# Graph attention on one core: group 1's values go into the banks of its own t, and group 0's transposes are split, reordered and paired

## The reference

```
h      = max(layernorm(x), 0)
out    = h @ weight;   q = h @ wq;   k = h @ wk
alpha  = max(q @ k^T, 0) * (adj != 0)
alpha  = softmax(alpha, axis=1)            # over the rows n of alpha[n, m]
result = x + alpha @ out
```

## Time and profile before

| | |
|---|---|
| median of 3 runs | 421.62 us (420.26 to 421.87) |
| the profiled execution, its own time | 420.8 us |
| span of its trace, first to last instruction | 419.0 us |
| PE busy | 406.6 us, 97% |
| DVE, ACT, POOL busy | 68%, 60%, 71% |

### The profile page before, as it was taken

The page is one execution under the profiler, slowest core; times in us unless marked ns, Lnnn a source line. Parts: engine busy times, 40 slices in busy tenths (PEclk is TensorE's granted clock), DMA queues, the critical chain, the costliest instruction groups (busy, mean ns, idle before and its releaser), DMA issues.

```text
span 419.0 us, 9187 instructions
## 1 busy us (share of the span) xinstructions
PE 406.6 (97%) x3499; PEld 314.8 (75%) x3499; DVE 282.9 (68%) x504; ACT 253.3 (60%) x517; POOL 298.2 (71%) x315
## 2 busy tenths in 40 slices
PE   5999997999999999999999999999999999999996
PEld 4434543779889797979889797979889797978452
DVE  4786566475866768685876768676777677456353
ACT  4478774657485666667485666667586765523421
POOL 0379887979979797979879797979889796130320
PEclk9999999999999999999999999999999999999999
DMA  7965748996969797896978598996988599261022
GB/s 286 364 91 97 194 81 212 202 219 177 191 216 178 221 165 206 199 210 178 196 238 157 154 213 219 194 207 180 187 251 151 157 228 221 51 107 59 0 103 100
DMA packets 157368, 73.97 MB, mean 177 GB/s; under 512 B 131216, under 2 KB 139408, under 8 KB 157328
## 3 DMA queue, kind: packets, MB, share of 16 engines
q1 hardware_dynamic: 156752, 72.37, 75.5%
q10 hardware_dynamic: 576, 1.05, 0.7%
HBM read 24.12 MB, written 16.78 MB: 98 GB/s over the span
## 4 chain that ended last, share of the span: by engine, by line
PE 81%; POOL 9%; DMA 3%; DVE 3%; ACT 1%; SPq 1%; issue 1%; DVEq 0%; POOLq 0%; ACTq 0%
PE bank L1041 9%; PE bank L1027 9%; PE bank L1026 9%; PE bank L1042 9%; PE bank L1024 9%; PE bank L1039 9%; PE s_bank L1055 3%; PE s_bank L1053 3%; PE s_bank L1054 3%; POOL hn_lo L375 2%; PE bank L1060 2%; PE bank L1062 2%; PE bank L1061 2%; DMA x_sb<-in_x 2%; POOL hn_lo L401 2%; PE bank L1160 2%
## 5 line engine op out<-in xcount | busy, mean ns | idle before, releaser
L375 POOL TENSOR_TENSOR hn_lo<-h,hn_hi 128x512 f16<-128x512 f32 x64 | 73.4, 1159 | 41.0 <-ACT hn_hi L512 40.7
L502 ACT ACTIVATE h<-x_sb,shift,rstd 128x512 f32<-128x512 f32 x64 | 49.8, 803 | 51.4 <-POOL shift L370 51.4
L401 POOL TENSOR_TENSOR hn_lo<-s,hn_hi 128x512 f16<-128x512 f32 x52 | 58.6, 1159 | 0.0
L1024 PE MATMUL bank<-hT_hi,mt_hi 128*128 128x256 f16 x208 | 56.7, 273 | 0.0
L1027 PE MATMUL bank<-hT_hi,mt_lo 128*128 128x256 f16 x208 | 56.7, 273 | 0.0
L1041 PE MATMUL bank<-wt_lo,hT_hi 128*128 128x256 f16 x208 | 56.7, 273 | 0.0
L1042 PE MATMUL bank<-wt_hi,hT_lo 128*128 128x256 f16 x208 | 56.7, 273 | 0.0
L1026 PE MATMUL bank<-hT_lo,mt_hi 128*128 128x256 f16 x208 | 56.7, 273 | 0.0
L1039 PE MATMUL bank<-wt_hi,hT_hi 128*128 128x256 f16 x208 | 56.7, 273 | 0.0
L517 ACT ACTIVATE hn_hi<-s 128x512 f16<-128x512 f32 x52 | 32.5, 628 | 36.4 <-POOL s L390 23.9
L407 POOL TENSOR_TENSOR probs<-exps,row_inv 128x512 f32<-128x512 f32 x16 | 16.8, 1049 | 47.3 <-DVE row_inv L829 47.3
(11 more groups left out here) (142 smaller groups left out, 1153.4 us busy)
## 6 DMA issues: line engine op xcount, KB each, us to landing
x_sb<-in_x SPq DMA_DIRECT2D x16, 1024.0 KB, 5.5
out_h<-x_sb SPq DMA_DIRECT2D x64, 256.0 KB, 2.1
adj_sb<-in_adj SPq DMA_DIRECT2D x16, 256.0 KB, 5.4
w_sb<-in_L_gnn_weight SPq DMA_DIRECT2D x1, 1024.0 KB, 11.4
hn_lo<-in_L_gnn_wk ACTq DMA_DIRECT2D x2, 256.0 KB, 3.9
hn_lo<-in_L_gnn_wk SPq DMA_DIRECT2D x2, 256.0 KB, 3.7
hn_hi<-in_L_gnn_wq SPq DMA_DIRECT2D x2, 256.0 KB, 6.3
hn_hi<-in_L_gnn_wq ACTq DMA_DIRECT2D x2, 256.0 KB, 6.9
```

What stands on the lines that cost most here:

```text
L375: nc.gpsimd.tensor_tensor(hn_lo[:, s, b], h[:, b], hn_hi[:, s, b], ALU.subtract).then_inc(h_split, 1)
L401: nc.gpsimd.tensor_tensor(low, s32[:, f], high, ALU.subtract).then_inc(s_split, 1)
L502: nc.scalar.activation(h[:, b], x_sb[:, s, b], ACT.Relu, bias=shift[:, b:b + 1], scale=rstd[:, b:b + 1]).then_inc(h_made, 1)
L1024: nc.tensor.matmul(o, bh[:, k, cols], ah[:, :, k], start=first and c == 0 and k == 0, stop=False, skip_group_check=True)
```

## The change

Three edits. First, group 1's values go to `M_BANK`, the banks where its t was; PE awaits each bank's `t_split` (the low part of t has been taken) before it writes v there, and `out_read` only ahead of scores(1); `period(2)` starts when seven of the eight values have been split. Second, SP awaits only the high part of h of graphs 0 and 1 to transpose it, then the low part; graphs 2 and 3 are transposed as a pair, high parts in one DMA and low parts in another. Third, on ACT the high part of t(1, 3) is made before those of the sums S2 and S4 of group 2, no longer after them.

```diff
-        V_BANK = [bank[VB][:], bank[VE][:], bank[FREE][:], bank[TA][:]]
+        def v_bank(g):
+            return M_BANK if g == 1 else [bank[VB][:], bank[VE][:], bank[FREE][:], bank[TA][:]]
...
-        hT0_landed = [sem(f"hT0_landed{b}") for b in range(GB)]
+        hT0_landed = [sem(f"hT0_landed{b}") for b in range(3)]
...
-            def transpose_first(b):
-                sp.wait_ge(h_split, b + 1)
-                sp.dma_start_transpose(hT_hi[:, 0, b], hn_hi[:, 0, b]).then_inc(hT0_landed[b], 16)
-                sp.dma_start_transpose(hT_lo[:, 0, b], hn_lo[:, 0, b]).then_inc(hT0_landed[b], 16)
+            def transpose_first(b, n, landed):
+                sp.wait_ge(h_hi_made, b + n)
+                sp.dma_start_transpose(hT_hi[:, 0, b:b + n].rearrange("p b k n -> p (b k) n"),
+                                       hn_hi[:, 0, b:b + n].rearrange("p b d -> p (b d)")).then_inc(landed, 16)
+                sp.wait_ge(h_split, b + n)
+                sp.dma_start_transpose(hT_lo[:, 0, b:b + n].rearrange("p b k n -> p (b k) n"),
+                                       hn_lo[:, 0, b:b + n].rearrange("p b d -> p (b d)")).then_inc(landed, 16)
...
-            for b in range(GB):
-                transpose_first(b)
+            transpose_first(0, 1, hT0_landed[0])
+            transpose_first(1, 1, hT0_landed[1])
+            transpose_first(2, 2, hT0_landed[2])
...
-            act.wait_ge(hT0_landed[3], 2 * 16)
             hi_of_h(2, 0, 3)
...
             hi_of_whole_t(1, 2)
+            hi_of_whole_t(1, 3)
             hi_of_sum(2, 0, 2, S2)
             hi_of_sum(2, 0, 3, S4)
-            hi_of_whole_t(1, 3)
             hi_of_whole_v(1, 0)
...
-            pe.wait_ge(hT0_landed[GB - 1], 2 * 16)
             pe.wait_ge(m_split, K)
...
-            pe.wait_ge(t_split, K + 1)
             for b in range(GB):
-                pe.wait_ge(out_read, b + 1)
+                pe.wait_ge(t_split, K + b + 1)
                 whole_product_v(1, b)
+            pe.wait_ge(out_read, GB)
             scores(1, 1, quadrants=False)
-            pe.wait_ge(v_split, 2 * GB)
+            pe.wait_ge(v_split, GB + TE + 1)
```

More of the change, by code:

```diff
@@ L601, in hi_of_whole_v @@
                     act.wait_ge(out_filled, GB * g)
-                nc.scalar.activation(v_hi[:, b], V_BANK[b], ACT.Copy, scale=T_SCALE).then_inc(v_hi_made, 1)
+                nc.scalar.activation(v_hi[:, b], v_bank(g)[b], ACT.Copy, scale=T_SCALE).then_inc(v_hi_made, 1)
             def hi_of_whole_t(g, c):
@@ L873, in lo_of_whole_v @@
                 vec.wait_ge(v_hi_made, GB * g + b + 1)
-                nc.vector.scalar_tensor_tensor(v_lo[:, b], V_BANK[b], T_SCALE, v_hi[:, b], ALU.mult,
+                nc.vector.scalar_tensor_tensor(v_lo[:, b], v_bank(g)[b], T_SCALE, v_hi[:, b], ALU.mult,
                                                ALU.subtract).then_inc(v_split, 1)
@@ L1143, in whole_product_v @@
             def whole_product_v(g, b):
-                s, dst = g % 2, V_BANK[b]
+                s, dst = g % 2, v_bank(g)[b]
                 for k in range(K):
```

## The result

The changed kernel takes 422.19 us in the median (421.61 to 422.71, 22 runs), the kernel before 421.38 us (420.26 to 422.13, 22 runs). The ratio is 1.0018, with a 95% interval of 1.0012 to 1.0025: slower by 0.2%, as small as predicted, and measurable only because there were so many runs. The profiled execution of the changed kernel took 422.03 us with a span of 420.2, the one of the kernel before 420.8 with 419.0. Lines after the change lie 7 or 8 higher: L409 is the old L401, L984 the old L977.

The account below looks back on a forecast made before the run. POOL's chain to p_lo(1), not PE, was taken as the bound: +1.35 (three L401) - 0.29 (layernorm scales) - 0.2 (earlier start) = +0.86 us, giving 422.5 us against the median 421.62; range 419.8 to 423.6 for 8 times in 10.

Parts of the forecast that it names:

- Part 1: Banks of v(1): removes PE waits of 2.67 and 0.40 us, worth 0 on the chain to the end.
- What bounds: POOL's chain from normalise(0) to p_lo(1) sets outs(1); the end moves by what p_lo(1) moves; PE's waits are covered.
- Part 2: Transposes: PE gains 1.0 us at v(0, 2), POOL's chain 0.2 us, bounds 0 and 1.0.
- the lower bound of the prediction: SP's queue: issuing a pair of transposes costs between 1.27 us (as one) and 2.54 us (as two).
- With a normal landing: Pair's DMA: landing normally, it leaves over half a microsecond to spare, so PE gains 1.0 us.
- Part 3: ACT's order: mt_lo start at 63.4 beside POOL's L401; three L401 lengthen, +1.35 us, layernorm scales change by -0.29.
- The price: Each mt_lo meeting a POOL L401 lengthens POOL's next by 0.45 us, bounds 0 and 0.68.
- The count: Group 2's L401 on POOL: numbers 2, 3 and 4 are lengthened, the first mt_lo falling inside the first.
- The sum: shift(3): +1.35 - 0.29 - 0.2 = +0.86 us, moving outs(1) from 89.75 to about 90.6 and the end with it.
- Free meetings: Rival: mt_lo beside POOL's L401 don't meet or cost POOL nothing; 420.5 us, or 419.7; chance 0.20.
- PE's waits as the bound: Rival: POOL has room, so PE's 4.1 us of waits come out in full; 417.5 us; chance 0.08.
- The pair lands late: Rival: the paired low transpose lands 1 us after 31.27, normalise(0) slips 1 us; 423.7 us; chance 0.12.

Follow-up runs that it names:

- e8: Changed kernel with graphs 2 and 3 transposed singly, four mt_lo held behind POOL's layernorm scales, two wt_lo moved earlier: 419.61 us, ratio 0.9954 to the kernel before.
- e2: Kernel before with only the four mt_lo held back behind POOL's layernorm scales of group 3: 421.35 us, ratio 0.9999.
- e4: Kernel before with only ACT's new order, t(1, 3)'s high part ahead of the sums S2 and S4: 423.27 us, ratio 1.0042.
- e9: Kernel before with only the new transposes, high parts first and graphs 2 and 3 as a pair: 421.53 us, ratio 1.0007.
- e6: Kernel before with only the new banks for v of group 1 and PE's waits for them: 421.20 us, ratio 1.0004.
- e1: Changed kernel with the four mt_lo held back behind POOL's layernorm scales of group 3: 420.61 us, ratio 0.9982 to the kernel before.
- e3: Changed kernel with ACT's old order, t(1, 3)'s high part behind the sums S2 and S4: 421.05 us, ratio 0.9998 to the kernel before.
- e7: Changed kernel with graphs 2 and 3 transposed each by itself, high parts still first: 421.12 us, ratio 1.0004 to the kernel before.
- e5: Changed kernel with the old first transposes, new banks and ACT order kept: 421.45 us, ratio 1.0010 to the kernel before.
- e10: Changed kernel with unpaired transposes and two of the four mt_lo held behind POOL's layernorm scales: 420.63 us, ratio 0.9987 to the kernel before.

## Why the prediction was right

Time and sign came out, and so did the mechanism on POOL, with one term too large and one missing. That the median fits as well as it does is in part luck: Part 1's zero holds only while PE keeps its full clock.

**What bounds.** Right for the profiled executions: `outs(1)` follows p_lo(1) by 0.05 us in both kernels, and what stands behind it takes PE the same 324.82 us. The waits that went from PE (2.67 and 0.40) came back as 2.17, 0.67 and a longer stand at `outs(1)`. e8, whose POOL chain is 0.62 shorter than that of the kernel before, is faster. In e2, e4 and e9, though, whose clock fell in mid-stream, PE was the last at `outs(1)`.

**Part 1, worth 0.** Right at full clock: in e6 `outs(1)` is at 90.10, not earlier than 89.75, and the 0.35 later are the lost first place of L367. What the prediction left out is what such a wait can do in other executions: in the profiles of e2 and e9 the granted clock falls behind it, and PE is as late as POOL at `outs(1)`, or later. There, removing the wait has a value ("Against the median" and the last section).

**Part 2, 1.0 us for PE and 0.2 for the chain.** The chain's 0.21 fits by luck. Counted from the first high part of h, `normalise(0)` comes 0.38 earlier, and all profiles agree: 35.86 to 35.95 us in the five with the old transposes, 35.48 in the four with the pair. The changed kernel's profile merely started 0.18 later. The softmax shift still takes 0.58 us (0.54 before), beside POOL as the prediction had it. PE's 1.0 didn't come: it restarts at 31.06 instead of 31.32, 0.44 earlier when counted from the same point. The queue of SP and the chain of waits in the changed kernel, 18 to 32 us:

```profile
24.79 1.31 SPq L281 DMA_TRANSPOSE hT_hi<-hn_hi  x1
26.14 1.34 SPq L284 DMA_TRANSPOSE hT_lo<-hn_lo  x1
```

```profile
26.14 4.88 DMA hT_lo<-hn_lo
```

A pair costs one issue (1.34, the lower bound of the prediction), so it is issued 1.00 us earlier than in the earlier trace rows, but lands 4.88 us later instead of 4.12. "With a normal landing" was the wrong assumption, 0.76 us slower (4.62 to 4.64 us in e1, e3 and e9, against 4.12 to 4.44 for the same transpose without the pair). It didn't matter, since PE's microsecond was hidden in any case.

**Part 3, +1.35 and -0.29.** The price was right: 1.61 - 1.16 = 0.45 for each L409 that follows an `mt_lo`. The count was wrong. I put the first `mt_lo` at 63.4 inside the first L401, which ends at 63.5; it came at 63.73, inside the second, since the low part of t(1, 3) waited for ACT until 60.48 and not 60.2. So two were lengthened, +0.90, and two `mt_lo` were left for the scales, which stayed at 2.96 (+0.02) instead of losing 0.29. The sum is 0.92 against 1.06 foreseen. e7, where the `mt_lo` come 0.3 us earlier against POOL's stream, has the three (+1.38) and the scales at 2.64 (-0.30) of the prediction, and the chain longer by 1.04.

The Trainium skill (SBUF — State Buffer, "Who interferes with whom") was right that a VectorE `tensor_tensor` with two inputs in SBUF contends with GpSimd's reads. The price by its whole duration would be 0.68 for each; the traces show 0.45, for the loop's kind as for this one.

**The sum.** `outs(1)` moved by +0.66 (foreseen +0.86), or by +0.48 without the 0.18 by which this profile started late: +0.87 on the chain, -0.38 ahead of it. The 0.59 at the end stood in no step: I had written that the end moves by what p_lo(1) moves. In the profiles that makes +1.26 against +0.9.

**Against the median.** Here another error offset the missing 0.59. The timed executions beside the experiments have their mean granted clock on record. Of the 29 of the kernel before that ran beside e1 to e4, 10 ran at 1.000, with a median of 420.6 us, and 19 at 0.994 to 0.996, with 421.5. Beside e5 to e8 the two kinds have 420.9 and 421.4, beside e9 and e10 421.0 and 421.4. The profile that I read was of the first kind (clock 1.000, 420.8 us). The changed kernel has both kinds too, 15 of 22 at 0.994 to 0.997, but they are no slower: 422.18 against 422.24 at full clock. So against executions at full clock the change costs 1.2 to 1.7 us, against the more frequent others 0.7 to 0.8, and the medians differ by 0.81. The clocks of the 22 executions of the kernel before that this last number rests on aren't on record.

**The rivals.** Free meetings: refuted by 1.61 and by e1. PE's waits as the bound: refuted at full clock, by e6 and by the 1.03 us that PE now waits for p_lo(1); where the clock fell behind `out_read`, PE was the bound, by 0.62 us in e9. Of the 4.1 us that this rival named, less than one was at stake in such executions. The pair lands late: true of the DMA, not of `normalise(0)`.

## What to carry to other kernels

Before an edit that lets an engine start earlier, write down what the other engines do at its new time: here an instruction with two SBUF operands on DVE cost POOL's chain 0.45 us a meeting, and putting it behind the neighbour's critical stretch (e1, e8) made a faster kernel of it (e8, which also drops the pair and moves two `wt_lo`: 0.46% below the one before). A wait removed from PE is worth what the chain behind the next join allows, in this kernel nothing at full clock; a covered wait can still cost, when the granted clock falls behind it. Times from the start of a span are compared between two profiles only after a look at an instruction ahead of all edits. An effect of half a microsecond needs the ends of both traces compared, not only the place of the edit.

## What the runs showed that I had not expected

**The granted clock falls after a wait in mid-stream.** In e2, PE stood still for 2.65 us in its wait for `out_read`; first PE's timeline, then the windows of e2:

```profile
65.89 0.38 PE L1151 MATMUL bank<-w_hi,hT_hi 128*128 128x512 f16 x1 [2.65 <-DVE x_sb L833]
```

```profile
65.00:68.00 3.00, 2.11 (x8) 0.95 (x9) 3.00 (x6) 0.00 (x0) 3.00 (x5) 0.82 1.01 178
68.00:71.00 3.00, 3.00 (x10) 1.07 (x9) 0.23 (x2) 0.76 (x2) 1.58 (x4) 0.61 0.79 150
```

In 68 to 71 us PE makes 10 matmuls instead of 14 (at half clock they start 0.43 us apart, otherwise 0.22) and the mean clock is 0.61: part of the stretch ran at the lower level, 1.2 GHz. In e4 the wait was 4.15 us, first in PE's timeline and then by windows:

```profile
80.21 0.40 PE L1024 MATMUL bank<-hT_hi,m_hi 128*128 128x256 f16 x1 [4.15 <-DVE v_lo L874]
```

```profile
80.00:83.00 3.00, 2.79 (x14) 1.99 (x15) 1.68 (x4) 0.63 (x1) 2.92 (x3) 0.50 1.11 333
83.00:86.00 3.00, 3.00 (x17) 2.19 (x16) 1.29 (x2) 2.90 (x10) 3.00 (x4) 0.54 1.26 276
```

Here it fell while PE still stood (77 to 80 us: 0.82). Four more profiles have such a stretch: e9 behind a wait of 2.98 us for `out_read`, and e3, e7 and e10 behind waits of 2.00, 2.60 and 2.05 us before `period(2)`. First e9, then e7, by windows:

```profile
65.00:68.00 3.00, 3.00 (x9) 1.12 (x8) 3.00 (x6) 0.00 (x0) 2.92 (x5) 0.53 0.66 140
```

```profile
79.00:82.00 3.00, 3.00 (x19) 2.26 (x18) 1.78 (x4) 0.63 (x1) 2.92 (x3) 0.62 1.14 311
```

These six executions have a mean clock of 0.992 to 0.996 on record, the six profiled ones without such a stretch 0.999 or 1.000, though three of them have waits of 2.67, 2.17 and 2.12 us (before, after, e5). So the same wait does it in some executions and not in others, and a mean of 0.996 or less marks those where it did.

What it costs depends on where it falls. Behind `out_read` (e2, e9) PE takes 25.24 and 25.20 us from v(1, 0) to `outs(1)` without a wait, in the kernel before 24.42 with 0.56 of waits in it: PE becomes the bound, and by these numbers the kernel before would reach `outs(1)` 0.8 us later in such an execution (my estimate; the two kinds of its executions differ by 0.9, 0.5 and 0.4 us in the three sets). Before `period(2)` (e3, e7, e10) it costs nothing: PE waited another 0.47 to 0.49 us at `outs(1)`, which still follows p_lo(1) by 0.05 or 0.06. The changed kernel has its longest wait, 2.17 us, before `period(2)`, and 0.67 and 1.03 us of waits behind it. That its 15 executions at lower mean clock lost it there, and those of the kernel before behind `out_read`, is likely, not shown: only their mean clocks are known.

**An int32-to-bf16 mask takes part in the meetings**: 0.42 us alone, 1.37 beside POOL, and POOL's instruction longer by 0.17 to 0.22 (e1, e10), less than half an `mt_lo`'s price.

**The pair, at 26 us, makes the end 0.56 to 0.60 us later at 415 us.** It has two issues fewer on SP, and in all four kernels with it an instruction packet travels beside the last store. The other eight have one packet more ahead of the last matmul, 10.8 to 11.9 us before it starts. How the pair moves the packet, and whether the packet delays the store, isn't shown.
